# A four-layer graph network kernel: 128-column products, the second batch-norm product and the scatter in plain fp32 instead of split fp32r, and the first constants moved into the work list

## What is computed

```python
x = _layernorm(x + _L0_gnn_ref(x, adj, ...))   # 8 Euler steps of a diffusion equation on the graph
x = _layernorm(x + _L1_gnn_ref(x, adj, ...))   # two graph convolutions, then 4 short LSTMs over windows of 1..4 nodes
x = _layernorm(x + _L2_gnn_ref(x, adj, ...))   # aggregation, 128 -> 256, batch norm, relu, 256 -> 128, batch norm
x = _layernorm(x + _L3_gnn_ref(x, adj, ...))   # attention over 256 edges, segment softmax, scatter to the source nodes
```

```python
# L1: first graph convolution (its product with Wg0 is the one that changes)
h = relu(einsum('ts,bsh->bth', adj, x @ Wg0 + bg0))
# L2: second product, between the two batch norms
h = relu(_batchnorm(x @ W1.T + b1, g1, be1)); out = h @ W2.T + b2; out = _batchnorm(out, g2, be2)
# L3: with Xq = H @ W_lin.T and Xv = H @ W_val.T
e = einsum('behd,hd->beh', leaky_relu(Xq[:, src] + Xq[:, dst]), a) + log(A0[src, dst] + EPS)
Y = segment_sum(softmax_by_source(e) * Xv[:, dst], src);  return Y @ W_out.T
```

## Time and profile before

| | |
|---|---|
| three timed runs | 1132.41, 1137.34, 1137.36 us; median 1137.34 us |
| profiled execution | 1132.74 us, its span 1131.0 us (1.7 us lie around the span) |
| mean granted TensorE clock | 0.938 of full speed |
| busy | PE 975.1 us (86%), DVE 696.4 (62%), ACT 573.7 (51%), POOL 341.5 (30%) |

### The profile page before, as it was taken

The page is one execution under the profiler, slowest core; times in us unless marked ns, Lnnn a source line. Parts: engine busy times, 40 slices in busy tenths (PEclk is TensorE's granted clock), DMA queues, the critical chain, the costliest instruction groups (busy, mean ns, idle before and its releaser), DMA issues. The chain is left out here.

```text
span 1131.0 us, 15450 instructions
## 1 busy us (share of the span) xinstructions
PE 975.1 (86%) x5376; PEld 842.2 (74%) x5376; DVE 696.4 (62%) x1576; ACT 573.7 (51%) x1199; POOL 341.5 (30%) x389
## 2 busy tenths in 40 slices
PE   4995999989998999999999999899899766289594
PEld 2673998778897889898789998787788644166474
DVE  4743344435555746655755665688778688644686
ACT  2112232465555565554655464566675486754256
POOL 0001131222332223331323332233332264553256
PEclk9987999999999999999999999999899988599797
DMA  7003001000100010101010103010100000000004
GB/s 200 1 1 73 19 19 75 20 20 1 38 11 28 1 38 20 38 1 39 1 38 19 39 1 110 2 38 20 38 19 1 1 1 0 0 1 1 0 20 130
DMA packets 34140, 31.64 MB, mean 28 GB/s; under 512 B 8594, under 2 KB 28178, under 8 KB 34068
## 3 DMA queue, kind: packets, MB, share of 16 engines
q1 hardware_dynamic: 33108, 30.64, 8.8%
q10 hardware_dynamic: 960, 0.07, 0.1%
HBM read 22.83 MB, written 7.87 MB: 27 GB/s over the span
## 5 line engine op out<-in xcount | busy, mean ns | idle before, releaser
L1366 ACT ACTIVATE gates<-psum,gbias 128x256 f32<-128x256 f32 (+2 forms) x312 | 157.8, 566 | 47.0 <-PE psum L67 43.8
L65 PE MATMUL psum<-LS,WI 128*128 128x256 f32 (+2 forms) x312 | 106.4, 341 | 12.3 <-ACT gates L1366 8.5
L72 POOL TENSOR_TENSOR LS<-A,LS 128x512 fp32r<-128x512 f32 (+2 forms) x44 | 47.9, 1089 | 199.3 <-ACT LS L1351 199.3
L66 PE MATMUL psum<-LS,WI 128*128 128x256 f32 (+2 forms) x312 | 104.8, 336 | 0.0
L67 PE MATMUL psum<-LS,WI 128*128 128x256 f32 (+2 forms) x312 | 104.7, 336 | 0.0
L72 DVE TENSOR_TENSOR yl<-psum,yh 128x512 fp32r<-128x512 f32 x74 | 50.8, 690 | 78.9 <-ACT yh L1308 42.5
L72 POOL TENSOR_TENSOR LS<-Hodd,LS 128x512 fp32r<-128x512 f32 (+2 forms) x44 | 48.6, 1104 | 168.1 <-ACT LS L1351 168.1
L65 PEld LDWEIGHTS psum<-LS,WI 128*128 128x128 f32 x312 | 61.2, 196 | 23.3 <-POOL LS L72 10.8
L65 PE MATMUL psum<-B2h,LT2h 128*128 128x256 f32 x256 | 72.7, 284 | 1.6 <-DVE X L1472 1.6
L67 PE MATMUL psum<-B2h,LT2l 128*128 128x256 f32 x256 | 72.4, 283 | 0.0
L66 PE MATMUL psum<-B2l,LT2h 128*128 128x256 f32 x256 | 72.4, 283 | 0.0
(11 more groups left out here) (408 smaller groups left out, 2975.8 us busy)
## 6 DMA issues: line engine op xcount, KB each, us to landing
WI<-lstm_weights SPq DMA_DIRECT2D x14, 512.0 KB, 3.6
WH<-lstm_weights SPq DMA_DIRECT2D x11, 512.0 KB, 4.5
X<-in_x SPq DMA_DIRECT2D x16, 256.0 KB, 5.0
out<-X SPq DMA_DIRECT2D x32, 128.0 KB, 1.9
lstm_weights<-WI SPq DMA_DIRECT2D x4, 512.0 KB, 2.6
lstm_weights<-WH SPq DMA_DIRECT2D x3, 512.0 KB, 2.6
A<-in_adj SPq DMA_DIRECT2D x1, 1024.0 KB, 6.1
z_A<-in_adj SPq DMA_DIRECT2D x1, 1024.0 KB, 5.2
```

Source lines behind the costliest of these rows:

```text
L65: pe.matmul(out, lhs[0], rhs[0], start=start, stop=False)
L66: pe.matmul(out, lhs[0], rhs[1], start=False, stop=False)
L72: return eng.tensor_tensor(out, full, high.bitcast(F32), ALU.subtract)
L1366: act.activation(gates[:, gate, 0:n], sh.psum[:, gate, 0:n], ACT.Tanh if gate == G else ACT.Sigmoid, bias=gbias[:, p_ - 1, gate:gate + 1]) ...
```

## The change

Three things.

First, these products lose the splits and become plain fp32 matmuls (two records each): the product with `Wg0` (128 columns), the second batch-norm product (512 columns), in attention the three products behind the gather (256 and 128 columns), the scatter (512 columns) and the projection (128 columns). With them go ACT's and DVE's splits of their operands: one copy out of PSUM, or none, is left. In `second` of the batch norm POOL has nothing left to do, ACT no longer copies results out, and DVE adds the bias on the way out of PSUM; in the gather DVE copies z out of PSUM (`Z`), and ACT brings u and v out in one instruction (`UV`).

Second, ACT's and DVE's heads in `phase_main` move into the list: item `("own", 0)` makes `ones` and `diag` (no DMA needed), item `("own", 1)` the rest, with the waits for `g_in` and `b_in`; both stand in `prologue()` behind the first sample's `back(0, 0)`, and the product of `ones` and `diag` (set item 4) behind `back(0, 1)`. The old item `("own",)` is now called `("dia",)`.

Third, the planner reckons 88 instead of 132 for a `("v", q, b, 0)` item.

```diff
-    sh.aWT = (room("aWTh", [P, 3, P], F32R), room("aWTl", [P, 3, P], F32R))
+    sh.aWT = room("aWT", [P, 3, P])
     sh.kept = at[0]
-    sh.WT = (room("WTh", [P, 2 * J, P], F32R), room("WTl", [P, 2 * J, P], F32R))
+    sh.WT = (room("WTh", [P, J, P], F32R), room("WTl", [P, J, P], F32R))
+    sh.W2T = room("W2T", [P, J, P])
...
+        here = nc.sbuf_base
         yh = sb("yh", [P, BABY, N], F32R)
+        mixes0 = nc.alloc_sbuf_tensor_at("mixes0", [P, BABY, N], F32, offset=here)
...
-            parts = [split(0, 0), split(0, 1), taps(0, 0)[:1], sets[0:C + 1], taps(0, 0)[1:], split(0, 2), taps(0, 1),
-                     split(0, 3), back(0, 0), taps(0, 2), back(0, 1), [next(late)], giant("t", 0, 0), taps(0, 3),
+            parts = [split(0, 0), split(0, 1), taps(0, 0)[:1], sets[0:C], taps(0, 0)[1:], split(0, 2), taps(0, 1),
+                     split(0, 3), back(0, 0), [("own", 0)], taps(0, 2), [("own", 1)], back(0, 1), sets[C:C + 1],
+                     [next(late)], giant("t", 0, 0), taps(0, 3),
...
-                return 132 if item[3] == 0 else 68
+                return 88 if item[3] == 0 else 68
...
-                        ins = product(pe, bank(n)[:, cols], (ych[:, m, cols], ycl[:, m, cols]),
-                                      (Wgs[0][0][:, :], Wgs[0][1][:, :]))
+                        ins = pe.matmul(bank(n)[:, cols], mixes0[:, m, cols], Wg0[:, :], start=True, stop=True)
                 else:
-                    ins = product(pe, bank(n), (Wgs[1][0][:, :], Wgs[1][1][:, :]), (ych[:, m, :], ycl[:, m, :]))
+                    ins = product(pe, bank(n), (Wg1h[:, :], Wg1l[:, :]), (ych[:, m, :], ycl[:, m, :]))
...
-            act.wait_ge(S["g_in"], 64)
-            for i in (0, 1):
-                act.activation(Wgs[i][0][:, :], Wg[i], ACT.Copy).then_inc(S["wg_hi"], 1)
+            def conv_weights():
+                act.wait_ge(S["g_in"], 64)
+                act.activation(Wg1h[:, :], Wg1, ACT.Copy).then_inc(S["wg_hi"], 1)
...
+            def conv_mixed(q, b, layer):
+                name, m = ("c", q, b, layer), mixed(q, b, layer)
+                n = ring[name]
+                if layer == 0:
+                    dve.wait_ge(S["ring_mm"], n + 1)
+                    dve.tensor_copy(mixes0[:, m, :], bank(n)).then_inc(S["ring_free"], 1)
...
-            dve.wait_ge(S["g_in"], 64)
-            dve.memset(ones, 1.0)
-            for c in range(C):
-                ins = dve.tensor_scalar(diag[:, c, :], sh.ident[:, :], rs[:, c:c + 1], None, ALU.mult)
-            ins.then_inc(S["ones_done"], 1)
-            for c in range(C):
-                ins = dve.tensor_scalar(RB0[:, c, :], bg0, rs[:, c:c + 1], None, ALU.mult)
-            link(ins)
-            for i in (0, 1):
-                dve.wait_ge(S["wg_hi"], i + 1)
-                ins = low_part(dve, Wgs[i][1][:, :], Wg[i], Wgs[i][0][:, :])
-            ins.then_inc(S["wg_done"], 1)
-            dve.wait_ge(S["b_in"], 32)
-            dve.tensor_tensor(gbias[:, :, :], bi[:, :, :], bh[:, :, :], ALU.add).then_inc(S["gbias_done"], 1)
+            def row_sum_diagonal():
+                dve.memset(ones, 1.0)
+                for c in range(C):
+                    ins = dve.tensor_scalar(diag[:, c, :], sh.ident[:, :], rs[:, c:c + 1], None, ALU.mult)
+                ins.then_inc(S["ones_done"], 1)
+
+            def conv_constants():
+                dve.wait_ge(S["g_in"], 64)
+                for c in range(C):
+                    ins = dve.tensor_scalar(RB0[:, c, :], bg0, rs[:, c:c + 1], None, ALU.mult)
+                link(ins)
+                dve.wait_ge(S["wg_hi"], 1)
+                low_part(dve, Wg1l[:, :], Wg1, Wg1h[:, :]).then_inc(S["wg_done"], 1)
+                dve.wait_ge(S["b_in"], 32)
+                dve.tensor_tensor(gbias[:, :, :], bi[:, :, :], bh[:, :, :], ALU.add).then_inc(S["gbias_done"], 1)
...
+                elif item == ("own", 0):
+                    row_sum_diagonal()
+                elif item == ("own", 1):
+                    conv_constants()
...
-                    pe.wait_ge(S["t_lo"], n + 1)
-                    pe.wait_ge(S["t_lo1"], n + 1)
                     wait(pe, S["o_out"], n - QB + 1)
                     for j in range(J):
-                        ins = product(pe, sh.psum[:, 4 + b, :], (WT[0][:, J + j, :], WT[1][:, J + j, :]),
-                                      (parts[0][J * b + j], parts[1][J * b + j]), start=(j == 0),
-                                      stop=(j == J - 1))
+                        pe.wait_ge(S["u_done"], J * n + j + 1)
+                        ins = pe.matmul(sh.psum[:, 4 + b, :], sh.W2T[:, j, :], U[:, J * b + j, :], start=(j == 0),
+                                        stop=(j == J - 1))
...
-                    wait(act, S["t_lo"], n - 1)
-                    wait(act, S["t_lo1"], n - 1)
+                    wait(act, S["o_mm"], n - QB + 1)
                     for j in range(J):
-                        act.activation(tmp[:, J * (b % 2) + j, :], H1[:, bass.ds(n, 1), j, :].rearrange("p o n -> p (o n)"), ACT.Relu,
-                                       bias=bsh[:, j:j + 1], scale=bsc[:, j:j + 1]).then_inc(S["u_done"], 1)
-                    if not isinstance(i, int) or n >= 2:
-                        second_out(n - 2, (b - 2) % QB)
+                        act.activation(U[:, J * b + j, :], H1[:, bass.ds(n, 1), j, :].rearrange("p o n -> p (o n)"),
+                                       ACT.Relu, bias=bsh[:, j:j + 1], scale=bsc[:, j:j + 1]).then_inc(S["u_done"], 1)
...
-                    wait(dve, S["o_mm"], n - QB + 1)
-                    for j in range(J):
-                        dve.wait_ge(S["u_done"], J * n + j + 1)
-                        dve.tensor_copy(parts[0][J * b + j], tmp[:, J * (b % 2) + j, :]).then_inc(S["t_hi"], 1)
-                    dve.wait_ge(S["t_hi"], J * n + 1)
-                    low_part(dve, parts[1][J * b], tmp[:, J * (b % 2), :], parts[0][J * b]).then_inc(S["t_lo"], 1)
-                    if not isinstance(i, int) or n >= 3:
-                        second_stats(n - 3)
+                    dve.wait_ge(S["o_mm"], n + 1)
+                    dve.tensor_scalar(O2[:, bass.ds(n, 1), :], sh.psum[:, 4 + b, :], par2[:, 0, 0:1], None, ALU.add)\
+                        .then_inc(S["o_out"], 1)
+                    if not isinstance(i, int) or n >= 1:
+                        second_stats(n - 1)
...
-                    for j in range(1, J):
-                        pool.wait_ge(S["t_hi"], J * n + j + 1)
-                        ins = low_part(pool, parts[1][J * b + j], tmp[:, J * (b % 2) + j, :], parts[0][J * b + j])
-                    ins.then_inc(S["t_lo1"], 1)
...
-                    act.wait_ge(S["z_mm"], n + 1)
-                    act.activation(ZH[:, s, :], sh.psum[:, s, :], ACT.Copy).then_inc(S["z_hi"], 1)
                     if not last:
+                        act.wait_ge(S["z_mm"], n + 1)
...
-                    wait(act, S["lr_done"], QB * g + 2 * h)
-                    act.activation(uq[:, s, :], sh.psum[:, 2 + s, 0:NE], ACT.Copy).then_inc(S["uv_out"], 1)
-                    act.activation(V[:, bass.ds(n, 1), :, :],
-                                   sh.psum[:, 2 + s, NE:2 * NE].rearrange("p (k d) -> p k d", k=K), ACT.Copy)\
-                        .then_inc(S["uv_out"], 1)
+                    act.activation(UV[:, bass.ds(n, 1), :], sh.psum[:, 2 + s, :], ACT.Copy).then_inc(S["uv_out"], 1)
...
-                    act.activation(vah[:, b, :, :], va[:, b, :, :], ACT.Copy).then_inc(S["va_hi"], 1)
...
-                    dve.wait_ge(S["z_hi"], n + 1)
-                    low_part(dve, ZL[:, s, :], sh.psum[:, s, :], ZH[:, s, :]).then_inc(S["z_lo"], 1)
+                    dve.wait_ge(S["z_mm"], n + 1)
+                    dve.tensor_copy(Z[:, s, :], sh.psum[:, s, :]).then_inc(S["z_out"], 1)
...
-                    weighted_low(n, b)
-                    if not first or b >= 2:
-                        scattered_low(n - 2, (b - 2) % QB)
...
-                        pe.wait_ge(S["z_lo"], n + s + 1)
-                        product(pe, sh.psum[:, 2 + s, 0:NE], (WT[0][:, 0, :], WT[1][:, 0, :]),
-                                (ZH[:, s, 0:NE], ZL[:, s, 0:NE]))
+                        pe.wait_ge(S["z_out"], n + s + 1)
+                        pe.matmul(sh.psum[:, 2 + s, 0:NE], WT[:, 0, :], Z[:, s, 0:NE], start=True, stop=True)
                         for k in range(K):
                             cols = slice(NE + k * P, NE + (k + 1) * P)
-                            ins = product(pe, sh.psum[:, 2 + s, cols], (ZH[:, s, cols], ZL[:, s, cols]),
-                                          (WT[0][:, 1, :], WT[1][:, 1, :]))
+                            ins = pe.matmul(sh.psum[:, 2 + s, cols], Z[:, s, cols], WT[:, 1, :], start=True, stop=True)
...
-                    ins = product(pe, sh.psum[:, 4 + b, cols], (ZH[:, b, cols], ZL[:, b, cols]),
-                                  (WT[0][:, 2, :], WT[1][:, 2, :]))
```

(27 more changed lines are left out.)

101 lines of the change are left out of this document (38 added, 63 removed).

## The result

The changed kernel takes 1098.41 us (median of four runs, 1097.57 to 1099.72), the kernel before 1135.92 us in the same comparison: a ratio of 0.9675, 95% interval 0.9648 to 0.9702. The forecast was 1098. The profiled execution took 1098.17 us with a span of 1096.4, against 1131.0: 34.6 us less.

What follows compares the result with a forecast made beforehand. TensorE bounds the main stage; elsewhere waits and chains do. Prologue -14.6, main -6, `second` -9.5, gather -5.9, attend 0 sum to -36.0: 1132.74 to 1096.7, called 1098 with half the 4.6 us profile-to-median gap; range 1087 to 1112.

Steps and rivals of the forecast that it cites:

- -15.5: Prologue: the second sample's transposes come at 95.5 instead of 111.08, before 0.9 us for the moved `cell,gates` product.
- rival 1: Prologue gains little, another wait replacing the 12.55 us; up to 12 of 14.6 us lost, 1110; chance 0.10.
- the forecast's 111 to 113: Prologue: time in us when DVE reaches its moved wait for `bh`, with the DMA landed, costing 0 us.
- rival 4: Prologue taps run at half rate for 6.8 us, half of it lost: +3.4 us, 1101; chance 0.10.
- 64 x 0.11 = 7.2 us off TensorE, at a busy share of 94.5%, so 0.945 x 7.2 = 6.8: Main stage: saving from four 128-column products for each of 16 samples; term taken as -6 us.
- rival 2: Main stage gives its gain back, 6 to 8 us; sign: busy time falls, idle time rises; chance 0.15.
- the 5.4 to 8.8 of the forecast: `second`: us TensorE works at half rate, costing 2.7 to 4.4 us within a -9.5 us term.
- the -0.67 us a pair: Gather: period falls from 8.12 to 7.45 us a pair; eight pairs and the first's double gain make -5.9.
- The split's 0.63: Gather: DVE copies z straight out of PSUM where ACT's `ZH` ran first, -0.63 us a pair.
- the product's 0.14: Gather: the product between z and uv, shorter by 0.11 x 2 and longer by 0.08, -0.14 us a pair.
- Forecast at nothing: Attend: 0 us, TensorE replacing DVE as the bound, 2.60 us a sample against 2.67; bounds -2 and +4.
- Rival 3: `second` and attend: wide fp32 products bound at half clock, 1161 with both; chance 0.04 both, 0.04 one.

Runs made afterwards that it cites:

- The extra product: Changed kernel with one more plain fp32 matmul of 512 columns a sample in the batch norm's `second`: 1115.39 us in one run.
- The scatter experiments: Changed kernel with the scatter split again, projection plain: one of its two products (k = 0, by DVE) 1093.69 us; both (by ACT and DVE) 1096.15 us.

## Why the prediction was right

**Prologue.** Right in mechanism and size (-15.5 against -15.8). DVE's wait for `bh` at its new place is gone, as the row at 118.33 shows; rival 1 did not come. DVE came there later than the forecast's 111 to 113, by the 2.5 us of the stage before and because 36 products of 384 columns (103.6 to 109.9) stood between the taps. Nor did rival 4: the taps behind the 16 transposes ran at the full clock's step of 0.23 us. The Trainium skill, page "TensorE: Matmul & The Clock Gate", section "Part 4: PE-mode transpose", says that transposes do not count as TensorE work in the way that products do; this is one more row against reading that as a loss here. But the 256-column products before the transposes could have kept the clock up too, so the transposes' own part stays open.

**Main stage.** The direction was right, the working was not. The failing step is "64 x 0.11 = 7.2 us off TensorE, at a busy share of 94.5%, so 0.945 x 7.2 = 6.8": it took the share of busy time for the share of products that bound. (64 x 0.11 is 7.0, a slip of little weight.) The price was nearly right: four products take 1.29 us split and 0.89 plain, 0.10 each. But at two of the places where eight of them stand together, the next thing is a wait for DVE's `B2l`, which grows by what the products save. The kernel before there:

```profile
345.35 0.22 PE L65 MATMUL psum<-Wg0h,yh 128*128 128x128 f32 x1
...
349.50 0.77 PE L65 MATMUL psum<-ATh,B2h 128*128 128x512 f32 x1 [1.35 <-DVE B2l L1545]
```

From the first product to the next work pass 349.50 - 345.35 = 4.15 us; in the changed kernel 333.80 - 329.65 = 4.15. Nothing is saved there. Summed over all places, first product to next matmul, it is 27.0 us before and 22.8 after: 4.3 us and not 6.8.

TensorE's busy time in the stage fell by 15.6 us (748.6 to 733.0) and its idle time rose by 6.9 (46.7 to 53.6), most of it in the two waits shown above (17.6 to 24.6 us). That is the sign that the prediction named for rival 2, and the waits did take a part of the gain back; the rival's price, the whole gain lost, did not come.

The stretch nevertheless shrank by 8.6, and by 8.1 between the two profiles with split products and 132 (mean 796.2) and the eight with plain ones (mean 788.1, 785.7 to 790.3). What is left beside the 4.3 goes with the clock. By the granted clock in the traces, TensorE stood at half clock in this stretch for 38.1 us in both of the former, and for 14.1 to 24.4 us in the eight, among which a stage is 0.37 us longer for each us at half clock (correlation 0.76). For the 17 us by which the means differ that is some 6 us, an estimate, which with 4.3 is 2 us more than the 8.1 measured, within what eight profiles can tell. Every profile with plain products has less time at half clock than those two. But the kernel before with 88 has 27.4 us of it and is shorter by about what the same slope gives for the 10.7 us less, so it is not the plain products alone that do it. Why there is less was not settled: no run here tells the products' doing from that of the waits' new places.

**`second`.** Right in mechanism and size. The extra product showed the bound directly. TensorE stood at half clock for the first 5.5 us of its work, which is inside the 5.4 to 8.8 of the forecast.

**Gather.** The failing step is the -0.67 us a pair. From the end of z to the next pair before: 0.20 to ACT's `ZH`, 1.37 to the product, 1.28 to `uq`, 0.42 to `lr`, 1.02 to the next pair. After: 0.20, 0.74, 1.28, 0.74, 1.02. The split's 0.63 came off as forecast, but `uv` costs 0.32 and not 0.20 (an ACT operation of 0.60 and a handover), and the product's 0.14 did not arrive: its records save 0.1, and its handover to ACT takes as much longer. That makes -0.31. The four steady pairs therefore gained 1.2 us and not 2.7. The first pair gained 0.16 and not 1.3. The second lost 1.0, since TensorE fell to half clock at 969.2 for 3.4 us; in three of the variants this did not happen and their second pair took 7.4 to 7.6 us. The last two pairs with the softmax tail gained 2.7, where the forecast had 2.2 with the earlier start of attend. (The counts of three matmuls of 256 and six of 128 columns given with the kernel before are for one sample, not for a pair; the prediction's working has them right.)

**Attend.** Forecast at nothing, and nothing it was, for the reason given: DVE's bound of 2.67 gave way to TensorE's of 2.61, forecast 2.60. The scatter experiments show that this zero is a sum of two parts: the projection gains 2.2 us and the plain scatter loses 2.4.

**`phase_operators`.** No term, and +2.5 us in the profile. The code is the same, and the difference goes with the clock: the granted clock was at half for 17.1 us of this stage, 10.2 before. Whether that is chance stays open. In the ten other profiles the stage ends between 87.2 and 90.1, but the two kernels without the list move have the two earliest ends (87.2 and 87.5) and the nine with it lie at 88.5 to 90.1.

**From the sum to the time.** The prediction puts half of the 4.6 us between profile and median on its 1096.7 and says 1098, where that makes 1099.0. In the result the profile (1098.17) lay only 0.2 us under its median (1098.41), and the profiles differ by 34.6 us and not by 36.0. That the two meet at 1098 is luck too.

Rival 3, the wide products at half clock throughout, did not come: `second` ran at half clock only up to 890.7, and at full clock behind it (mean granted clock 1.00 from there to 917.6), with TensorE busy for 24.9 of 26.9 us.

## What to carry to other kernels

Plain fp32 against a three-pass split is a question of width and place: per product it saved 0.10 us at 128 columns and cost 0.17 at 512, so it paid at 512 only where the split itself stood on the chain (`second`, where POOL's part of it did), and not in the scatter. Before multiplying a saving by a stage's busy share, look at what follows each of the shortened pieces: where it is a wait for another engine, the saving can end there. And before crediting a stage's gain to an edit, compare the time at half clock: in the gather the same code took 7.61 us for a pair at full clock and 9.15 with 3.4 us of it at half. A head that waits for DMAs ahead of a work list holds up all of the list, also those items that need none of it; moving it behind the first items was worth 16 us here, with no arithmetic changed.

## What the runs showed of the hardware beyond what was expected

The same main stage, instruction for instruction, spent 14.1 to 24.4 us at half clock in seven profiles, and its length moved between 785.7 and 790.3 us with it. Differences under some 5 us between kernels of this size can't be read from one execution. A plain fp32 group of eight records of 128 columns took 0.89 us, 0.11 each, about the step of an fp32r matmul of that width (twelve in 1.29 us).
